# Inverse root mean squares of the second layer's q and k: one GpSimd power operation in place of eleven VectorE links

## The chip, the cores and the metric

The kernel runs on one core of a Trainium2 chip. A core has a matrix engine (TensorE, PE in the profile), three engines for elementwise work (VectorE, DVE; ScalarE, ACT; GpSimd, POOL) and a queue for transfers (SyncE, SP). Each works down its own list of instructions in order; semaphores tie the lists together. The metric is the device time in microseconds (us); less is better.

## What is computed

Two transformer layers on 16 sequences ("batches" here) of 512 tokens with 128 features, 16 heads of 8 features. The part that the change touches is the normalisation of q and k in the second layer: each head's 8 values are divided by the root of their mean square.

```python
def rms_norm(x, w):
    xf = x.astype(jnp.float32)
    rms = jnp.sqrt(jnp.mean(xf * xf, axis=-1, keepdims=True) + EPS)
    return (xf / rms * w.astype(jnp.float32)).astype(x.dtype)
...
q = rms_norm(q, qn_w)
k = rms_norm(k, kn_w)
scores = jnp.einsum('bhsd,bhtd->bhst', q, k) * scale
attn = jax.nn.softmax(scores, axis=-1)
out = jnp.einsum('bhst,bhtd->bhsd', attn, v)
...
x = x + _L0_attn_ref(_layernorm(x), ...)
x = x + _L0_ffn_ref(_layernorm(x), ...)
x = x + _L1_attn_ref(_layernorm(x), ...)
x = x + _L1_ffn_ref(_layernorm(x), ...)
```

## The kernel before, in words

**Tiling and stages.** 32 attention passes follow each other: layer 0 and layer 1 of the 16 batches, interleaved as (0, b), (1, b-2). A pass is 64 units. One unit is a score tile of 128x512 for the exponential (TensorE, then `exp` on ScalarE into `probs`) and, 26 units ahead, a score tile for the row maxima (TensorE, then a maximum reduction on VectorE into `neg_max`). After each four units TensorE multiplies `probs` with the values. There are three score banks for each of the two uses, so TensorE can be at most three tiles ahead of VectorE or ScalarE. Everything else (projections, norms, the gated network, routing) is cut into pieces and put between the units.

**What sets the order.** Each engine has a table of due times, in units: `PE_AT`, `ACT_AT`, `DVE_AT`, `POOL_AT`, `SP_AT`. A program loop over `TIMES` writes the instructions of an engine in the order of these times; at run time only semaphores and the list itself hold an instruction. A due time is therefore a place in a list and no clock time: an engine that has nothing ahead starts as soon as its semaphores allow.

**q and k of the second layer.** TensorE computes them by token (`qka`, `qkb`), VectorE adds a bias into `qk1` (`take_qk1`), ScalarE squares them into `sq`, which lies in the buffer `ht`. `inverse_rms` on VectorE then does 14 steps, `nw0` to `nw13` in the table: two sums over 8 values (`ms`, 128x64 each), mean and epsilon, and eleven Newton links on 128x128 tiles (a shift, a subtraction for the first guess, three rounds of three). Each link waits for the one before by the semaphore `newton` and stands alone between two maxima. `scale_qk` on GpSimd multiplies `qk1` with the result `nw_y` in eight instructions, four for q and four for k. TensorE transposes the scaled q and k (pieces `qt` and `kt`, line L1125, `ps<-ident,qk` in the profile); ScalarE and GpSimd split them in bfloat16 parts (`part0`, `residual1`, `part1`, `residual2`), and SyncE sends the parts through memory into `q_stack` and `k_stack`, from which the next attention pass of layer 1 is fed.

**What stands around it on GpSimd.** `normalise` (L589) multiplies the attention output `o_raw`, in two halves, with the inverse denominators; these come by a transfer into `rden_all`, after a reciprocal on VectorE (L927). The half 0 of a pass stands ahead of the scaling, half 1 behind it. TensorE's projection `pr0` or `pr1` (L1201) waits for both. `norm_factors` (L570, L572) raises variances (`vpe`, 128x4) to the power -0.5 with the constant tile `half_neg` and multiplies; ScalarE's normalisation L696 waits for it. On VectorE `parts_high` (the cast L899) and `parts_low` (L908) stand after each sixteen maxima.

Of the kernel before, what the change touches and what calls it, by code (L numbers as in the profile page):

```python
# [7 lines left out]
I32 = mybir.dt.int32  # L8
ALU = mybir.AluOpType
ACT = mybir.ActivationFunctionType  # L10
AX = mybir.AxisListType

BATCH, SEQ, D = 16, 512, 128
HEADS, HD = 16, 8
TT = SEQ // 128
# [5 lines left out]
LN_EPS, RMS_EPS = 1e-5, 1e-6  # L21
# [57 lines left out]
SP_AT = {"A": {"rows0": -5, "rows1": 10, "rows2": 23, "rows3": 46, "den0": 40, "rden0": 55, "den1": 66,  # L79
                "rden1": 74},  # L80
# [40 lines left out]
PE_DUE, ACT_DUE, DVE_DUE, POOL_DUE, SP_DUE = (due_table([t]) for t in (PE_AT, ACT_AT, DVE_AT, POOL_AT, SP_AT))  # L121
# [5 lines left out]
def at(due, name, t):  # L127

    return due[name][t] if name in due and t in due[name] else None
# [51 lines left out]
def need(eng, sem, value):  # L181

    if value > 0:
        eng.wait_ge(sem, value)


def build(nc, T, out_dram):
    ctx = ExitStack()
    with ctx:
        def sb(name, shape, dt=F32):  # L190
            return ctx.enter_context(nc.sbuf_tensor(name, shape, dt))

        def sem(name):
            return ctx.enter_context(nc.semaphore(name))
# [23 lines left out]
        w_mid = sb("w_mid", [128, 2 * EXPERTS])  # L218
        mid_bias = sb("mid_bias", [128, 2 * EXPERTS])
        w_lora = sb("w_lora", [EXPERTS * RANK + 1, D])  # L220
        half_neg = sb("half_neg", [128, TT])

        x_in = sb("x_in", [128, TT, D])
        res = [[sb(f"res{l}{k}", [128, TT, D]) for k in range(l + 1)] for l in (0, 1)]
# [5 lines left out]
        vpe = [sb(f"vpe{k}", [128, TT]) for k in range(4)]  # L230
        rstd = [sb(f"rstd{k}", [128, TT]) for k in range(4)]
# [24 lines left out]
        qk1 = sb("qk1", [128, TT, 2 * D])  # L256
        sq = ht[:, 0:2, :].rearrange("p c (t n) -> p (c t) n", n=2 * D)
        ms = sb("ms", [128, TT * 32])
        nw_y = sb("nw_y", [128, TT * 32])
        nw_t = sb("nw_t", [128, TT * 32])  # L260
        nw_u = sb("nw_u", [128, TT * 32])

        rm = sb("rm", [128, TT, 2 * EXPERTS])
        lmax = sb("lmax", [128, TT])
# [48 lines left out]
        rstd_ready = [sem(f"rstd_ready{k}") for k in range(4)]  # L313
# [25 lines left out]
        tanh_done = sem("tanh_done")  # L339
        ht_done = sem("ht_done")  # L340
        squared = sem("squared")
        newton = sem("newton")
        qk_normed = [sem(f"{c}_normed") for c in "qk"]
        moe = sem("moe")
        l_exp = sem("l_exp")
# [1 line left out]
        gate_ready = sem("gate_ready")  # L347
        coef_ready = sem("coef_ready")
        stored = sem("stored")
        N_NEWTON = 14  # L350

        def v_of(l, b):
            return v_aug[l][b % 2 if l == 1 else 0]
# [192 lines left out]
        def _(pool):  # L546
# [20 lines left out]
            def norm_factors(k, b):  # L567

                pool.wait_ge(var_ready[k], b + 1)
                pool.tensor_tensor(rstd[k][:, :], vpe[k][:, :], half_neg[:, :], ALU.pow).then_inc(rstd_ready[k], 1)  # L570
                pool.wait_ge(rstd_ready[k], b + 1)
                pool.tensor_tensor(shift[k][:, :], neg_mean[k][:, :], rstd[k][:, :], ALU.mult).then_inc(shift_ready[k], 1)  # L572

# [12 lines left out]
            def normalise(l, c, b):  # L586
# [2 lines left out]
                pool.tensor_tensor(o_of(l, b)[:, c, :], o_of(l, b)[:, c, :], rden_all[:, c, :], ALU.mult  # L589
                                   ).then_inc(att_ready[l], 1)  # L590

            def scale_qk(n, b):

                if n == 0:
                    pool.wait_ge(newton, N_NEWTON * (b + 1))
                x = qk1[:, :, D * n:D * n + D].rearrange("p t (h e) -> p t h e", e=HD)
                inv = nw_y[:, :].rearrange("p (t n h) -> p t n h", t=TT, n=2)[:, :, n, :]
                for t in range(TT):
                    last = pool.tensor_tensor(x[:, t, :, :], x[:, t, :, :], wide(inv[:, t, :, None], 2, HD), ALU.mult)
                last.then_inc(qk_normed[n], 1)  # L600
# [25 lines left out]
            clear_values(v_aug[1][0], 2)  # L626
            clear_values(v_aug[1][1], 3)
            for t in TIMES:
                for n in (0, 1):
                    b = at(POOL_DUE, f"sc{n}", t)  # L630
                    if b is not None:
                        scale_qk(n, b)
                a = at(POOL_DUE, "no1", t)
                if a is not None:
                    normalise(a[0], 1, a[1])
                b = at(POOL_DUE, "nf1", t)
                if b is not None:
                    norm_factors(1, b)
                for c in range(NH):
                    b = at(POOL_DUE, f"um{c}", t)  # L640
                    if b is not None:
                        up_mul(c, b)
                for l in (1, 0):
                    for n in (0, 1):
                        b = at(POOL_DUE, f"r1_{'qk'[n]}{l}", t)
                        if b is not None:
                            residual1(l, n, b)
                        b = at(POOL_DUE, f"r2_{'qk'[n]}{l}", t)
                        if b is not None:
                            residual2(l, n, b)  # L650
                b = at(POOL_DUE, "nf3", t)
                if b is not None:
                    norm_factors(3, b)
                b = at(POOL_DUE, "mix", t)
                if b is not None:
                    mix(b)
                b = at(POOL_DUE, "nf0", t)
                if b is not None:
                    norm_factors(0, b)
                b = at(POOL_DUE, "nf2", t)  # L660
                if b is not None:
                    norm_factors(2, b)
                a = at(POOL_DUE, "no0", t)
                if a is not None:
                    normalise(a[0], 0, a[1])
# [177 lines left out]
        def _(dve):  # L843
# [110 lines left out]
                    last = dve.tensor_tensor(qk1[:, 2 * half + t, :], gen[:, 256 * t:256 * t + 256], qk1_bias[:, :], ALU.add)  # L954
                last.then_inc(read[name], 1)

            def inverse_rms(first, count, b):

                for n in range(first, first + count):
                    if n < 2:  # L960
                        dve.wait_ge(squared, 2 * b + n + 1)
                        op = dve.tensor_reduce(ms[:, 64 * n:64 * n + 64],
                                               sq[:, 2 * n:2 * n + 2, :].rearrange("p t (g e) -> p (t g) e", e=HD),
                                               AX.X, ALU.add)
                    else:
                        dve.wait_ge(newton, N_NEWTON * b + n)
                        if n == 2:
                            op = dve.tensor_scalar(ms[:, :], ms[:, :], 1.0 / HD, RMS_EPS, ALU.mult, ALU.add)
                        elif n == 3:
                            op = dve.tensor_scalar(nw_t[:, :].bitcast(I32), ms[:, :].bitcast(I32), 1, None,  # L970
                                                   ALU.logical_shift_right)
                        elif n == 4:
                            op = dve.tensor_scalar(nw_y[:, :].bitcast(I32), nw_t[:, :].bitcast(I32), -1.0,
                                                   float(0x5f3759df), ALU.mult, ALU.add)
                        elif n % 3 == 2:
                            op = dve.tensor_tensor(nw_t[:, :], nw_y[:, :], nw_y[:, :], ALU.mult)
                        elif n % 3 == 0:
                            op = dve.scalar_tensor_tensor(out=nw_u[:, :], in0=nw_t[:, :], scalar=-0.5, in1=ms[:, :],
                                                          op0=ALU.mult, op1=ALU.mult)
                        else:  # L980
                            op = dve.scalar_tensor_tensor(out=nw_y[:, :], in0=nw_u[:, :], scalar=1.5, in1=nw_y[:, :],
                                                          op0=ALU.add, op1=ALU.mult)
                    op.then_inc(newton, 1)

            def route(link, b):

# [41 lines left out]
            for t in TIMES:  # L1028
# [5 lines left out]
                a = max_at(t - 1)  # L1034
                if a is not None and a[2] % 16 == 15:
                    parts_low(a[0], a[2] // 16, a[1])
                for n in range(N_NEWTON):
                    b = at(DVE_DUE, f"nw{n}", t)
                    if b is not None:
                        inverse_rms(n, 1, b)  # L1040
                for l in (1, 0):
                    for part in (0, 1):
                        b = at(DVE_DUE, f"tv{l}{'ab'[part]}", t)
# [6 lines left out]
                b = at(DVE_DUE, "add1", t)  # L1050
                if b is not None:
                    project_add(1, x3, b)
                b = at(DVE_DUE, "st3a", t)
# [3 lines left out]
                b = at(DVE_DUE, "st3b", t)  # L1057
                if b is not None:
                    stats(3, x3, b, (2, 3))
                b = at(DVE_DUE, "mo3", t)  # L1060
                if b is not None:
                    moments(3, b)
                b = at(DVE_DUE, "fa3", t)
                if b is not None:
                    factors_in(3, b)
                for link in range(3):
                    b = at(DVE_DUE, f"ro{link}", t)
                    if b is not None:
                        route(link, b)
                for link in range(3):  # L1070
                    b = at(DVE_DUE, f"ga{link}", t)
                    if b is not None:
                        gates(link, b)
                b = at(DVE_DUE, "fin", t)
                if b is not None:
                    finish(b)
                b = at(DVE_DUE, "st0a", t)
# [3 lines left out]
                b = at(DVE_DUE, "st0b", t)  # L1081
# [237 lines left out]
```

## Time and profile before

| | us |
|---|---|
| median of three runs | 2039.22 |
| lowest and highest run | 2016.17, 2040.07 |
| the profiled execution's own time | 2025.97 |
| its span | 2024.2 |
| mean granted TensorE clock in it | 0.954 of 2.4 GHz |

The rows further down come from this one profiled execution. Times in them are us from the start of the span; durations of grouped instructions are means in ns. An instruction's duration begins before the one ahead of it on the same engine has quite ended, so that a row's end is up to 0.1 us behind the next row's start. "PEclk" is the granted clock of TensorE as a share of 2.4 GHz: 1.00 is 2.4 GHz and 0.50 is 1.2 GHz. Lines such as L893 are those of the kernel.

### The profile page before, as it was taken

The numbers are of one execution on the slowest core, as the hardware profiler recorded it, in microseconds if no ns is written. First come the engines' busy times: TensorE is split into PE (matmuls) and PEld (weight loads), VectorE is DVE, ScalarE is ACT, GpSimd is POOL, SyncE is SP. The second block draws the span as 40 slices with busy tenths as digits, with TensorE's granted clock in tenths as the row PEclk, the third lists the DMA queues.
The fourth block names the chain that finished last, engine by engine and source line by source line (L and its number), as shares of the span: only waits on it lengthen the run. The fifth ranks groups of instructions, "written<-read, shape, count | busy, mean of one in ns | idle before, by whom it ended". The sixth has DMA issues, their size and how long they took to land.

```text
span 2024.2 us, 32134 instructions
## 1 busy us (share of the span) xinstructions
PE 1763.1 (87%) x10958; PEld 650.9 (32%) x10958; DVE 1604.7 (79%) x3587; ACT 1431.4 (71%) x2921; POOL 438.1 (22%) x579
## 2 busy tenths in 40 slices
PE   4998898989989898998988889898988989898895
PEld 1232332323233232333333233332423323233233
DVE  3978786887988888787887969887797877786871
ACT  2777676776877777676786857777687776666773
POOL 3122112131222213112122311213121221222201
PEclk8899997999999999999999989999999989899987
DMA  6223405032050513205041240504205042022310
GB/s 120 59 71 82 99 24 137 18 114 51 24 146 14 140 27 87 79 24 142 18 120 46 63 103 13 148 18 111 54 23 143 18 112 48 19 80 59 80 34 22
DMA packets 162644, 141.34 MB, mean 70 GB/s; under 512 B 38761, under 2 KB 144050, under 8 KB 162482
## 3 DMA queue, kind: packets, MB, share of 16 engines
q1 hardware_dynamic: 162482, 139.29, 26.6%
q8 instruction: 88, 1.44, 0.3%
q14 instruction: 74, 0.61, 0.1%
HBM read 77.38 MB, written 55.57 MB: 66 GB/s over the span
## 4 chain that ended last, share of the span: by engine, by line
PE 36%; DVE 23%; DMA 14%; ACT 13%; issue 5%; SPq 5%; POOL 5%; DVEq 0%; POOLq 0%; ACTq 0%
DVE neg_max L893 15%; PE ps L1175 11%; PE ps L1160 7%; PE ps L1196 6%; ACT probs L690 6%; DMA rden_all<-rden_rows 4%; DMA q_stack<-m_parts 3%; DMA k_stack<-k_rows 3%; ACT xn L696 3%; PE ps L1149 3%; PE ps L1125 2%; PE ps L1240 2%; PE ps L1201 2%; DMA k_rows<-kp 2%; SPq L424 2%
## 5 line engine op out<-in xcount | busy, mean ns | idle before, releaser
L893 DVE TENSOR_REDUCE neg_max<-ps 128x1 f32<-128x512 f32 x2048 | 1314.9, 680 | 208.0 <-PE ps L1149 203.3
L690 ACT ACTIVATE probs<-ps 128x512 f32<-128x512 f32 x2048 | 1098.4, 595 | 362.6 <-PE ps L1160 361.6
L1149 PE MATMUL ps<-k_stack,q_stack 48*128 48x512 bf16 x2048 | 699.1, 397 | 81.2 <-DMA k_stack<-k_rows 38.7
L1160 PE MATMUL ps<-q_stack,k_stack 50*128 50x512 bf16 x2048 | 672.2, 393 | 76.5 <-ACT probs L690 31.2
L1175 PE MATMUL ps<-probs,v_aug 128*32 128x512 f32 x4096 | 567.6, 627 | 0.1
L1160 PEld LDWEIGHTS ps<-q_stack,k_stack 50*128 50x128 bf16 x2048 | 153.2, 94 | 614.6 <-ACT probs L690 386.4
L1149 PEld LDWEIGHTS ps<-k_stack,q_stack 48*128 48x128 bf16 x2048 | 157.5, 94 | 223.7 <-DVE neg_max L893 158.1
L589 POOL TENSOR_TENSOR o_raw<-o_raw,rden_all 128x512 f32<-128x512 f32 x64 | 81.7, 1276 | 664.9 <-DMA rden_all<-rden_rows 664.9
L1175 PEld LDWEIGHTS ps<-probs,v_aug 128*32 128x32 f32 x4096 | 81.6, 109 | 156.4 <-issue 110.0
L570 POOL TENSOR_TENSOR rstd<-vpe,half_neg 128x4 f32<-128x4 f32 x64 | 64.5, 1008 | 297.3 <-DVE vpe L884 297.3
L696 ACT ACTIVATE xn<-x,shift,rstd 128x128 f32<-128x128 f32 x192 | 81.0, 491 | 32.3 <-POOL shift L572 32.3
L613 POOL TENSOR_TENSOR coef<-gating,rm 128x64 f32<-128x64 bf16 x64 | 16.8, 295 | 329.8 <-DVE gating L1009 329.8
L606 POOL TENSOR_TENSOR ht<-up,gs 128x512 f32<-128x512 f32 x48 | 61.0, 1271 | 122.3 <-ACT up L671 122.3
L1201 PE MATMUL ps<-wo,o_raw 128*128 128x128 f32 x512 | 72.6, 300 | 12.9 <-POOL o_raw L589 12.3
L1201 PEld LDWEIGHTS ps<-wo,o_raw 128*128 128x128 f32 x512 | 66.3, 209 | 33.4 <-issue 32.3
L1125 PE MATMUL ps<-ident,xn 128*128 128x128 f32 x256 | 47.2, 313 | 32.4 <-ACT xn L696 30.7
L931 DVE TENSOR_TENSOR x<-ps,res 128x512 f32<-128x512 f32 x32 | 22.1, 691 | 61.6 <-PE ps L1201 61.6
L943 DVE SCALAR_TENSOR_TENSOR gs<-th,ps 128x512 f32<-128x512 f32 x48 | 33.0, 688 | 40.2 <-ACT th L740 38.2
L1196 PE MATMUL ps<-xnt,w_gate 128*128 128x256 f32 x192 | 54.3, 405 | 9.8 <-ACT xnt L671 3.7
L671 ACT ACTIVATE up<-ps 128x512 f32<-128x512 f32 x48 | 28.7, 597 | 47.4 <-PE ps L1196 47.4
L931 DVE TENSOR_TENSOR x<-ps,x 128x512 f32<-128x512 f32 x32 | 22.0, 688 | 45.4 <-PE ps L1240 28.3
L1196 PE MATMUL ps<-xnt,w_up 128*128 128x256 f32 x192 | 54.3, 405 | 2.8 <-DVE gs L943 2.6
(103 smaller groups left out, 1503.7 us busy)
## 6 DMA issues: line engine op xcount, KB each, us to landing
q_stack<-q_rows SPq DMA_DIRECT2D x128, 192.0 KB, 3.8
k_stack<-k_rows SPq DMA_DIRECT2D x128, 192.0 KB, 4.8
rden_all<-rden_rows SPq DMA_DIRECT2D x64, 256.0 KB
q_rows<-qp SPq DMA_DIRECT2D x32, 384.0 KB, 2.6
k_rows<-kp SPq DMA_DIRECT2D x32, 384.0 KB, 3.5
q_rows<-qp SPq DMA_DIRECT2D x32, 256.0 KB, 3.1
k_rows<-kp SPq DMA_DIRECT2D x32, 256.0 KB, 3.2
x_in<-in_L_attn_x SPq DMA_DIRECT2D x16, 256.0 KB, 3.1
```

The lines of the kernel that those rows point to most:

```text
L570: pool.tensor_tensor(rstd[k][:, :], vpe[k][:, :], half_neg[:, :], ALU.pow).then_inc(rstd_ready[k], 1)
L589: pool.tensor_tensor(o_of(l, b)[:, c, :], o_of(l, b)[:, c, :], rden_all[:, c, :], ALU.mult).then_inc(att_ready[l], 1)
L606: pool.tensor_tensor(ht[:, c, :], up[:, :], gs[:, :], ALU.mult).then_inc(ht_done, 1)
L690: act.activation(probs[:, g % RING, :], ps[:, g % BANKS, :], ACT.Exp).then_inc(exps, 1)
L696: last = act.activation(xn[k][:, t, :], x[:, t, :], ACT.Identity, bias=shift[k][:, t:t + 1], scale=rstd[k][:, t:t + 1])
L893: dve.tensor_reduce(neg_max[l][:, pair // 2, col:col + 1], ps[:, BANKS + g % BANKS, :], AX.X, ALU.max, negate=True).then_inc(max_taken, 1)
L1125: return pe.transpose(dst, src, ident[0:n, 0:n])
L1149: pe.matmul(ps[:, BANKS + g % BANKS, :], q_stack[l][row:row + KROWS, pair, tok:tok + 128], k_stack[l][row:row + KROWS, pair, :], start=Tru ...
L1160: pe.matmul(ps[:, g % BANKS, :], k_stack[l][row:row + AROWS, pair, tok:tok + 128], q_stack[l][row:row + AROWS, pair, :], start=True, stop= ...
L1175: last = pe.matmul(acc[32 * j:32 * j + 32, :], v_of(l, b)[:, kt, 8 * e + 2 * group + pp, :], probs[:, (g + j) % RING, :], start=(s == 0 an ...
L1196: return pe.matmul(gen[:, 256 * half:256 * half + 256], w, xt[:, 256 * half:256 * half + 256], start=True, stop=True)
L1201: last = pe.matmul(gen4[:, t, :], o_of(l, b)[:, c, 128 * t:128 * t + 128], wo[l][:, c, :], start=c == 0, stop=c == 1)
```

## The change

VectorE keeps the two sums and the step for mean and epsilon, now `ms0` to `ms2` in the table at the due times of the first three steps (55, 57, 59); the eleven links go. GpSimd gets one `tensor_tensor` with the operation power, `ms` (128x128) to the power of `half_neg`, into a new tile `inv_rms`. `half_neg` grows from 128x4 to 128x128 for it. The new operation's place in GpSimd's table is 3 of the group M2, ahead of the scaling at 7, and the scaling waits for its semaphore `inv_ready`. VectorE's first sum of the next batch waits for the same semaphore.

```diff
@@ -63,9 +63,7 @@
-                "mo2": 45, "tqa": 54, "tqb": 55, "nw0": 55, "nw1": 57, "nw2": 59, "nw3": 60, "nw4": 61,
...
+                "mo2": 45, "tqa": 54, "tqb": 55, "ms0": 55, "ms1": 57, "ms2": 59},
@@ -74,7 +72,7 @@
-           "M2": {"sc0": 7, "sc1": 7, "r1_q1": 11, "r2_q1": 22, "r1_k1": 19, "r2_k1": 22},
+           "M2": {"pw": 3, "sc0": 7, "sc1": 7, "r1_q1": 11, "r2_q1": 22, "r1_k1": 19, "r2_k1": 22},
@@ -218,7 +216,7 @@
-        half_neg = sb("half_neg", [128, TT])
+        half_neg = sb("half_neg", [128, TT * 32])
@@ -567,7 +564,7 @@
-                pool.tensor_tensor(rstd[k][:, :], vpe[k][:, :], half_neg[:, :], ALU.pow).then_inc(rstd_ready[k], 1)
+                pool.tensor_tensor(rstd[k][:, :], vpe[k][:, :], half_neg[:, 0:TT], ALU.pow).then_inc(rstd_ready[k], 1)
@@ -589,12 +586,16 @@
+            def inverse_rms(b):
+
+                pool.wait_ge(mean_sq, N_MS * (b + 1))
+                pool.tensor_tensor(inv_rms[:, :], ms[:, :], half_neg[:, :], ALU.pow).then_inc(inv_ready, 1)
+
             def scale_qk(n, b):
 
-                if n == 0:
-                    pool.wait_ge(newton, N_NEWTON * (b + 1))
+                pool.wait_ge(inv_ready, b + 1)
                 x = qk1[:, :, D * n:D * n + D].rearrange("p t (h e) -> p t h e", e=HD)
-                inv = nw_y[:, :].rearrange("p (t n h) -> p t n h", t=TT, n=2)[:, :, n, :]
+                inv = inv_rms[:, :].rearrange("p (t n h) -> p t n h", t=TT, n=2)[:, :, n, :]
@@ -954,33 +958,18 @@
-            def inverse_rms(first, count, b):
...
-                        elif n % 3 == 2:
-                            op = dve.tensor_tensor(nw_t[:, :], nw_y[:, :], nw_y[:, :], ALU.mult)
-                        elif n % 3 == 0:
-                            op = dve.scalar_tensor_tensor(out=nw_u[:, :], in0=nw_t[:, :], scalar=-0.5, in1=ms[:, :],
-                                                          op0=ALU.mult, op1=ALU.mult)
-                        else:
-                            op = dve.scalar_tensor_tensor(out=nw_y[:, :], in0=nw_u[:, :], scalar=1.5, in1=nw_y[:, :],
-                                                          op0=ALU.add, op1=ALU.mult)
-                    op.then_inc(newton, 1)
+            def mean_square(n, b):
+
+                if n < 2:
+                    dve.wait_ge(squared, 2 * b + n + 1)
+                    need(dve, inv_ready, b)
+                    op = dve.tensor_reduce(ms[:, 64 * n:64 * n + 64],
+                                           sq[:, 2 * n:2 * n + 2, :].rearrange("p t (g e) -> p (t g) e", e=HD),
+                                           AX.X, ALU.add)
+                else:
+                    dve.wait_ge(mean_sq, N_MS * b + n)
+                    op = dve.tensor_scalar(ms[:, :], ms[:, :], 1.0 / HD, RMS_EPS, ALU.mult, ALU.add)
+                op.then_inc(mean_sq, 1)
```

The first place where the order of instructions moves is GpSimd's list around the scaling. This is the list of before, in the middle of the program:

```order
L570 TENSOR_TENSOR rstd0<-vpe0,half_neg 128x4
L572 TENSOR_TENSOR shift0<-neg_mean0,rstd0 128x4
L589 TENSOR_TENSOR o_raw10<-o_raw10,rden_all 128x512
L599 TENSOR_TENSOR qk1<-qk1,nw_y 128x128 x8
L589 TENSOR_TENSOR o_raw10<-o_raw10,rden_all 128x512
L577 TENSOR_TENSOR qf1<-qf1,qp1 128x512
L577 TENSOR_TENSOR kf1<-kf1,kp1 128x512
```

And this is the same place in the changed kernel, whose line numbers are others:

```order
L567 TENSOR_TENSOR rstd0<-vpe0,half_neg 128x4
L569 TENSOR_TENSOR shift0<-neg_mean0,rstd0 128x4
L586 TENSOR_TENSOR o_raw10<-o_raw10,rden_all 128x512
L592 TENSOR_TENSOR inv_rms<-ms,half_neg 128x128
L600 TENSOR_TENSOR qk1<-qk1,inv_rms 128x128 x8
L586 TENSOR_TENSOR o_raw10<-o_raw10,rden_all 128x512
L574 TENSOR_TENSOR qf1<-qf1,qp1 128x512
```

The power stands between half 0 of `o_raw` and the scaling; half 1 and the splitting of q and k stay behind the scaling. The second place is VectorE's list between the sums of squares and the cast after sixteen maxima, in the kernel before:

```order
L968 TENSOR_SCALAR ms<-ms 128x128
L893 TENSOR_REDUCE neg_max0<-ps 128x1
L970 TENSOR_SCALAR nw_t<-ms 128x128
L893 TENSOR_REDUCE neg_max0<-ps 128x1
L973 TENSOR_SCALAR nw_y<-nw_t 128x128
L893 TENSOR_REDUCE neg_max0<-ps 128x1
L976 TENSOR_TENSOR nw_t<-nw_y 128x128
L893 TENSOR_REDUCE neg_max0<-ps 128x1
L978 SCALAR_TENSOR_TENSOR nw_u<-nw_t,ms 128x128
L893 TENSOR_REDUCE neg_max0<-ps 128x1
L981 SCALAR_TENSOR_TENSOR nw_y<-nw_u,nw_y 128x128
L893 TENSOR_REDUCE neg_max0<-ps 128x1 x2
```

In the changed kernel the same place reads:

```order
L971 TENSOR_SCALAR ms<-ms 128x128
L897 TENSOR_REDUCE neg_max0<-ps 128x1 x7
L931 RECIPROCAL rden1<-den1 128x32
L897 TENSOR_REDUCE neg_max0<-ps 128x1 x3
L903 CAST neg_high0<-neg_max0 128x16
```

The links between the maxima are gone. In the list of before the reciprocal L927 follows the last row shown, so five links stand ahead of it and six behind.

## Rows read from the trace of the kernel before

**Rows 1.** The page: busy time by engine, and the chain that ended last.

```profile
PE 1763.1 (87%) x10958; PEld 650.9 (32%) x10958; DVE 1604.7 (79%) x3587; ACT 1431.4 (71%) x2921; POOL 438.1 (22%) x579
...
PE 36%; DVE 23%; DMA 14%; ACT 13%; issue 5%; SPq 5%; POOL 5%; DVEq 0%; POOLq 0%; ACTq 0%
```

**Rows 2.** Busy time by stretch: stretch, length, then each engine, clock, DMA.

```profile
998.90:1011.70 12.80, 11.15 (x69) 2.83 (x67) 12.77 (x32) 9.60 (x21) 1.27 (x1) 1.00 0.07 24
```

**Rows 3.** The chain in order of time (start, us on the chain, what), batch 7.

```profile
999.70 0.13 DVE nw_t L970
...
1001.16 0.20 DVE nw_t L976
...
1010.24 0.79 DVE nw_u L978
```

**Rows 4.** Timeline of GpSimd, batch 7: start, us, operation, idle time before it.

```profile
1009.61 1.27 POOL L589 TENSOR_TENSOR o_raw<-o_raw,rden_all 128x512 f32<-128x512 f32 x1 [19.72 <-DMA rden_all<-rden_rows]
1011.91 2.96 POOL L599 TENSOR_TENSOR qk<-qk,nw_y 128x128 f32<-128x128 f32 x8 [1.02 <-DVE nw_y L981]
1029.08 1.27 POOL L589 TENSOR_TENSOR o_raw<-o_raw,rden_all 128x512 f32<-128x512 f32 x1 [14.20 <-DMA rden_all<-rden_rows]
```

**Rows 5.** Timeline of TensorE, batch 7: q taken, and the projection behind it.

```profile
1025.83 0.66 PE L1125 MATMUL ps<-ident,qk 128*128 128x128 f32 x4
...
1030.85 2.05 PE L1201 MATMUL ps<-wo,o_raw 128*128 128x128 f32 x16
```

**Rows 6.** GpSimd's groups by shape: count, busy us, mean ns, idle before and releaser.

```profile
L570 POOL TENSOR_TENSOR rstd<-vpe,half_neg 128x4 f32<-128x4 f32 x64 | 64.5, 1008 | 297.3 <-DVE vpe L884 297.3
L599 POOL TENSOR_TENSOR qk<-qk,nw_y 128x128 f32<-128x128 f32 x128 | 47.4, 411 | 42.6 <-DVE nw_y L981 42.6
L572 POOL TENSOR_TENSOR shift<-neg_mean,rstd 128x4 f32<-128x4 f32 x64 | 13.0, 203 | 5.0
```

**Rows 7.** Timelines of GpSimd and TensorE: scaling and q taken, batches 1 and 12.

```profile
283.94 1.14 POOL L599 TENSOR_TENSOR qk<-qk,nw_y 128x128 f32<-128x128 f32 x3 [1.02 <-DVE nw_y L981]
297.87 0.66 PE L1125 MATMUL ps<-ident,qk 128*128 128x128 f32 x4
...
1614.05 2.96 POOL L599 TENSOR_TENSOR qk<-qk,nw_y 128x128 f32<-128x128 f32 x8 [1.02 <-DVE nw_y L981]
1627.97 0.66 PE L1125 MATMUL ps<-ident,qk 128*128 128x128 f32 x4
```

**Rows 8.** Timeline of GpSimd, batch 13.

```profile
1737.28 2.96 POOL L599 TENSOR_TENSOR qk<-qk,nw_y 128x128 f32<-128x128 f32 x8 [1.02 <-DVE nw_y L981]
1746.28 1.01 POOL L570 TENSOR_TENSOR rstd<-vpe,half_neg 128x4 f32<-128x4 f32 x1 [6.03 <-DVE vpe L884]
```

**Rows 9.** Timeline of TensorE: two of its longest waits.

```profile
1165.89 0.61 PE L1149 MATMUL ps<-k_stack,q_stack 48*128 48x512 bf16 x2 [3.86 <-DMA k_stack<-k_rows]
...
1651.44 0.61 PE L1149 MATMUL ps<-k_stack,q_stack 48*128 48x512 bf16 x2 [4.43 <-DMA k_stack<-k_rows]
```

**Rows 10.** Maxima L893 by stretch: length, VectorE's time and count, granted clock, DMA.

```profile
1166.00:1182.00 16.00, 8.19 (x13) 0.50 0.48 144
1047.10:1063.10 16.00, 13.67 (x22) 1.00 0.63 177
1651.40:1660.00 8.60, 4.04 (x6) 0.50 0.90 241
```

**Rows 11.** Timelines of GpSimd and VectorE at 1038 us.

```profile
1038.31 1.16 POOL L583 TENSOR_TENSOR qp<-qf,qp 128x512 bf16<-128x512 f32 x1
1038.44 1.05 DVE L883 TENSOR_SCALAR neg_mean<-mv 128x4 f32<-128x4 f32 x1
```

**Rows 12.** Timelines of VectorE's cast and of GpSimd, two places.

```profile
1019.27 0.17 DVE L899 CAST neg_high<-neg_max 128x16 bf16<-128x16 f32 x1
...
1074.85 1.01 POOL L570 TENSOR_TENSOR rstd<-vpe,half_neg 128x4 f32<-128x4 f32 x1 [9.73 <-DVE vpe L884]
...
1075.40 0.17 DVE L899 CAST neg_high<-neg_max 128x16 bf16<-128x16 f32 x1
```

More of the change, by code:

```diff
@@ L258, in build @@
         ms = sb("ms", [128, TT * 32])
-        nw_y = sb("nw_y", [128, TT * 32])
-        nw_t = sb("nw_t", [128, TT * 32])
-        nw_u = sb("nw_u", [128, TT * 32])
+        inv_rms = sb("inv_rms", [128, TT * 32])
         rm = sb("rm", [128, TT, 2 * EXPERTS])
@@ L341, in build @@
         squared = sem("squared")
-        newton = sem("newton")
+        mean_sq = sem("mean_sq")
+        inv_ready = sem("inv_ready")
         qk_normed = [sem(f"{c}_normed") for c in "qk"]
@@ L349, in build @@
         stored = sem("stored")
-        N_NEWTON = 14
+        N_MS = 3
         def v_of(l, b):
@@ L628, in _ @@
             for t in TIMES:
+                b = at(POOL_DUE, "pw", t)
+                if b is not None:
+                    inverse_rms(b)
                 for n in (0, 1):
@@ L955, in take_qk1 @@
                 last.then_inc(read[name], 1)
-            def inverse_rms(first, count, b):
[L959 to L964, printed above, removed]
-                    else:
[L966 to L974, printed above, removed]
-                        elif n % 3 == 2:
-                            op = dve.tensor_tensor(nw_t[:, :], nw_y[:, :], nw_y[:, :], ALU.mult)
-                        elif n % 3 == 0:
-                            op = dve.scalar_tensor_tensor(out=nw_u[:, :], in0=nw_t[:, :], scalar=-0.5, in1=ms[:, :],
-                                                          op0=ALU.mult, op1=ALU.mult)
-                        else:
-                            op = dve.scalar_tensor_tensor(out=nw_y[:, :], in0=nw_u[:, :], scalar=1.5, in1=nw_y[:, :],
-                                                          op0=ALU.add, op1=ALU.mult)
-                    op.then_inc(newton, 1)
@@ L1036, in _ @@
                     parts_low(a[0], a[2] // 16, a[1])
-                for n in range(N_NEWTON):
-                    b = at(DVE_DUE, f"nw{n}", t)
+                for n in range(N_MS):
+                    b = at(DVE_DUE, f"ms{n}", t)
                     if b is not None:
-                        inverse_rms(n, 1, b)
+                        mean_square(n, b)
                 for l in (1, 0):
```

2 rows, old and new, of the table DVE_AT are left out of this document.

## Prediction

> **What bounds the kernel now.** I read the page first. Its busy line gives TensorE 87%, VectorE 79%, ScalarE 71% and GpSimd 22% of 2024.2 us, and the chain that ended last takes 36% of the span on TensorE, 23% on VectorE and only 5% on GpSimd [rows 1]. No engine bounds the whole: one unit of attention (one score tile for the maximum, one for the exponential) goes round TensorE, VectorE and ScalarE in turn, and every engine works down a fixed list. So a place decides, not an average.
>
> The change sits in two places. The first is the stretch of Newton links. From 998.9 to 1011.7 us (batch 7) VectorE is busy for 12.77 of 12.80 us, TensorE for 11.15, ScalarE for 9.60 [rows 2], and the chain in order of time runs here through VectorE: a maximum, a link of 0.13 or 0.20 us, a maximum, a link [rows 3]. Here a link costs the whole machine its time. The second place is the GpSimd list. It finishes `o_raw` of half 0 at 1009.61+1.27 = 1010.9, waits 1.02 us for the last link, scales q and k in 2.96 us, and then has nothing to do for 14.2 us [rows 4]. TensorE asks for the scaled q only at 1025.83 [rows 5].
>
> **What the change removes.** Eleven links per batch. On the chain an integer link holds VectorE for 0.13 us, a multiplying one for 0.20, and the one that runs into `o_raw` on GpSimd for 0.79 [rows 3]. Two of 0.13, eight of 0.20 and one of 0.79 make 2.65 us a batch, 42 us in all as an upper bound. TensorE is busy 11.15 of the 12.80 us, so it would soon bound the stretch itself: I take 35 us if nothing else changes, 25 to 42.
>
> **What it adds.** One power of 128x128 elements on GpSimd, a shape that the trace does not have. It has the same operation on 128x4: 1008 ns in the mean of 64 [rows 6]. A multiply of the same 128x4 takes 203 ns and one of 128x128 takes 411 [rows 6]; one of 128x512 takes 1.27 us [rows 4]. So GpSimd has a fixed part of about 0.2 us and a slope of some 2.1 ns an element, and the power costs 805 ns more than the multiply for four elements. The question is whether these 805 ns are paid once or per element.
> - Lower bound, paid once: 0.411+0.805 = 1.2 us.
> - Per element, 805/4 = 201 ns each: 0.411+128x0.201 = 26.2 us.
> - Upper bound, the whole 1008 ns in proportion: 32x1.008 = 32.3 us.
>
> I take 26.2. GpSimd's other operations differ in slope and hardly in their fixed part, so an operation that is this much dearer at four elements is dearer by its arithmetic, and arithmetic is done for each element. Nothing in the trace excludes a long start-up.
>
> **Where it lies.** The new operation stands behind `o_raw` of half 0 and ahead of the eight scalings and of `o_raw` of half 1 (the first excerpt of the order), so it starts at 1010.9, not when the mean squares are ready at 999.1. It ends at 1037.1, and the first four scalings (half of 2.96) at 1038.6. TensorE wants q at 1025.83: it stands for 12.8 us, and with it, since every list is in order, VectorE and ScalarE. `o_raw` of half 1 then ends at 1041.3; TensorE's next user of it came 5 us behind q in the old trace (1030.85 against 1025.83 [rows 5]) and comes at 1043.6 now, so this costs nothing more. Batches 1 to 12 all show this distance: in the first the scaling starts at 283.94 and q is taken at 297.87, in the last 1614.05 and 1627.97 [rows 7]. The break-even is a power of 14.95-1.5 = 13.4 us, about 100 ns an element: anything shorter is hidden and the kernel gains, anything longer is paid in full 16 times.
>
> In batch 13 the scaling starts at 1737.28 and so the power at about 1736.3, and the norm factors of another batch stand right behind (1746.28 [rows 8]). They would come at 1736.3+26.2+3.0 = 1765.5, 19 us late. ScalarE and TensorE take their result a few us later; with that slack I put 5 us more on this batch. For the first batch and the last two I take the same 12.8.
>
> So 16x12.8+5 = 210 us are lost. Of the removed links only those ahead of the chain to `o_raw` of half 0 still help, five a batch, those before the reciprocal of the denominators in VectorE's list (the second excerpt of the order): 2x0.13+3x0.20 = 0.86 us [rows 3], 14 us in all. The rest only lets TensorE arrive sooner at a wait. That leaves +196.
>
> **The clock after each stall.** A TensorE that stands loses clock. Where it waited 3.86 us (to 1165.89) and 4.43 us (to 1651.44) for `k_stack` [rows 9], the granted clock behind was 0.50, 1.2 GHz, for 16 and 8.6 us more [rows 10]. At 0.50 VectorE did 13 maxima in 16 us, and 22 at full clock in the same place of an earlier pair of batches [rows 10]: 41% of the pace is gone. A stall of 12.8 us is longer than either. I add the shorter one, 8.6x0.41 = 3.5 us, for each of 16, 56 us; the bounds are 0 and 16x0.41 = 6.6 a batch, 105 us.
>
> Sum: 196+56 = +252 against the profiled execution's own time, 2025.97 us: 2278. The three runs shown lie at 2016, 2039 and 2040, and the same sum on their median gives 2291; I say **2285**.
>
> **The rivals.**
> 1. *The power is cheap, and the kernel gets no slower.* The 805 ns are start-up; the operation ends before 1024.3. Then the links are simply gone: 2026-35 = 1991 us, between 1984 and 2001, 1.2 to 2% faster. It decides at 13.4 us of length. For it: four elements are a thin base to go by, and no row excludes a long start-up. Against it: the multiply's start-up, 0.2 us. [...]
> 2. *The long operation also blocks VectorE.* Some VectorE operations wait for GpSimd to finish: `neg_mean` took 1.05 us for four elements a partition when it met a 1.16 us operation of GpSimd, and both ended at 1039.5 [rows 11]. Yet next to a power that began at 1074.85 and took its 1.01 us a cast at 1075.40 took 0.17 [rows 12], as the cast at 1019.27 does that meets nothing. In batch 7 a cast stands at 1019.27 [rows 12], 8.4 us behind the start of the power. If it is held until the end, VectorE stands for 17.8 us and TensorE stops at most three maxima (2 us) later: 3 to 5 us more a batch, 48 to 80 in all, 2335 to 2365 us. The Trainium skill (Advanced Engine Details and Errata, GPSIMD Details) says that the two engines share a read and a write interface and conflict when VectorE uses two ports or two SBUF inputs; by it this happens, and the `neg_mean` row agrees.
> 3. *In between.* Part start-up, part slope, 13.4 to 22 us: 2030 to 2210.
>
> That the operation would not replace the links is excluded: the order shows all eleven gone and one power in each batch.
>
> **How the numbers follow.** Power of 22 us or more without a block 0.45, with a block 0.21, in between 0.14, cheap 0.20. The forecast is the first. A range of 2045 to 2400 leaves out the cheap case and a sliver at the top and holds about 0.8; the upper end is 2285 and the 32.3 us operation (6x16 = 98) and some of the block. The slow case alone would be 2200 to 2400. About 2% is what a measurement of this kernel can tell from no change. Slower by over 2%: 0.45+0.21 and 0.12 of the middle, 0.78. Within 2%: the rest of the middle and most of the cheap case, 0.15. Faster by over 2%: 0.07, the cheap case when all 42 us come out.
>
> **What would show it.** The new operation's row: its mean, above all above or below 13.4 us. The waits: TensorE at the transposes of `qk` on GpSimd, some 12 us for each batch; none if the power is cheap. The granted clock: the mean under 0.954, with low stretches that begin in these stalls. VectorE: casts of over 5 us mean the block. If TensorE's wait is there but much shorter than 12 us with a power of 26 us, I have misread where it starts.

## The result, and the profile after

The changed kernel is slower: 2122.85 us median of four runs (2120.86 to 2134.0) against 2027.7 us for the kernel before (four runs, 2014.74 to 2040.07). The ratio is 1.0455, 95% interval 1.0405 to 1.0506, some 92 us. The direction was forecast and the time lies within the range, which was wide, but the forecast was 2285 us, +252 on the profiled execution. The profiled execution after took 2123.08 us, 97 more than the one before: the forecast loss is 2.6 times the one that came. The lines below are from this execution.

The page of the changed kernel: busy time by engine, and the chain that ended last, by engine and by line.

```profile
PE 1763.1 (83%) x10958; PEld 653.2 (31%) x10958; DVE 1562.9 (74%) x3411; ACT 1431.5 (67%) x2921; POOL 769.6 (36%) x595
...
PE 33%; POOL 21%; ACT 15%; DVE 14%; DMA 10%; issue 5%; SPq 2%; DVEq 0%; POOLq 0%; ACTq 0%
POOL inv_rms L592 16%; PE ps L1164 9%; DVE neg_max L897 9%; ACT probs L694 7%; PE ps L1149 6%; PE ps L1185 5%; ACT xn L700 4%; PE ps L1114 3%; DMA rden_all<-rden_rows 3%; DMA q_stack<-m_parts 3%; PE ps L1138 2%; PE ps L1229 2%; PE ps L1190 2%; DMA k_stack<-k_rows 2%; DVE bn L873 2%
```

Against [rows 1], TensorE does the same work in a longer span, VectorE has 42 us less, GpSimd 331.5 more, and GpSimd goes from 5% to 21% of the chain, 16% of it the new power alone. The groups of the power by shape, from the same kernel (busy us, mean ns, idle before):

```profile
L592 POOL TENSOR_TENSOR inv_rms<-ms,half_neg 128x128 f32<-128x128 f32 x16 | 332.5, 20781 | 5.2 <-DVE ms L971 5.2
...
L567 POOL TENSOR_TENSOR rstd<-vpe,half_neg 128x4 f32<-128x4 f32 x64 | 64.5, 1007 | 293.6 <-DVE vpe L888 293.6
```

A power of 128x128 takes 20.78 us where I took 26.2 [rows 6]. (Measured from its start to the start of the scaling behind it, it is 20.85 to 20.87 us in all 16 batches.) Batch 7 on GpSimd's timeline (start, us, operation, idle before), the place of [rows 4]:

```profile
1056.45 1.27 POOL L586 TENSOR_TENSOR o_raw<-o_raw,rden_all 128x512 f32<-128x512 f32 x1 [18.85 <-DMA rden_all<-rden_rows]
1057.67 20.79 POOL L592 TENSOR_TENSOR inv_rms<-ms,half_neg 128x128 f32<-128x128 f32 x1
1078.54 2.95 POOL L600 TENSOR_TENSOR qk<-qk,inv_rms 128x128 f32<-128x128 f32 x8
1081.45 1.27 POOL L586 TENSOR_TENSOR o_raw<-o_raw,rden_all 128x512 f32<-128x512 f32 x1
```

And TensorE's timeline there, the place of [rows 5]: the last work before q, and q itself.

```profile
1070.20 1.06 PE L1164 MATMUL ps<-probs,v_aug 128*32 128x512 f32 x8
1080.18 1.09 PE L1114 MATMUL ps<-ident,qk 128*128 128x128 f32 x4 [8.91 <-POOL qk L600]
```

TensorE stands for 8.91 us. The view of waits has it for the whole kernel, with the waits for `k_stack` (total us, times, longest):

```profile
PE ps L1114 <- POOL qk L600: 134.0, 15, 9.5
...
PE ps L1138 <- DMA k_stack<-k_rows: 23.6, 15, 5.9
...
PE ps L1114 <- ACT m_parts L675: 18.2, 1, 18.2
```

The waits for `k_stack` in the kernel before:

```profile
PE ps L1149 <- DMA k_stack<-k_rows: 38.7, 14, 5.8
```

Fifteen stalls, 134 us; the sixteenth batch, 13, stalls elsewhere, for 18.2 us. That is 152 us of new standing for 97 us of time. So two things have to be explained: why the stalls are shorter than 12.8 us, and where 55 us went.

### The profile page after: what moved, and what is told of

Its sections match the earlier page's. It is cut to its first block, busy times and chain, and to the rows that moved or that the text cites. A ratio compares the mean times of both kernels' runs of the same rounds, so it can differ in the third digit from the quotient of the medians.

```text
span 2121.3 us, 32004 instructions
## 1 busy us (share of the span) xinstructions
PE 1763.1 (83%) x10958; PEld 653.2 (31%) x10958; DVE 1562.9 (74%) x3411; ACT 1431.5 (67%) x2921; POOL 769.6 (36%) x595
## 4 chain that ended last, share of the span: by engine, by line
PE 33%; POOL 21%; ACT 15%; DVE 14%; DMA 10%; issue 5%; SPq 2%; DVEq 0%; POOLq 0%; ACTq 0%
POOL inv_rms L592 16%; PE ps L1164 9%; DVE neg_max L897 9%; ACT probs L694 7%; PE ps L1149 6%; PE ps L1185 5%; ACT xn L700 4%; PE ps L1114 3%; DMA rden_all<-rden_rows 3%; DMA q_stack<-m_parts 3%; PE ps L1138 2%; PE ps L1229 2%; PE ps L1190 2%; DMA k_stack<-k_rows 2%; DVE bn L873 2%
## 5 line engine op out<-in xcount | busy, mean ns | idle before, releaser
L592 POOL TENSOR_TENSOR inv_rms<-ms,half_neg 128x128 f32<-128x128 f32 x16 | 332.5, 20781 | 5.2 <-DVE ms L971 5.2
L1114 PE MATMUL ps<-ident,qk 128*128 128x128 f32 x128 | 33.9, 417 | 134.4 <-POOL qk L600 134.0
L723 ACT ACTIVATE qf<-ps,qn_scaled 128x512 f32<-128x512 f32 x16 | 11.0, 687 | 139.0 <-PE ps L1114 139.0
L1114 PEld LDWEIGHTS ps<-ident,qk 128*128 128x128 f32 x128 | 22.0, 210 | 161.3 <-issue 148.9
```

The costliest lines, as they stand in the source:

```text
L592: pool.tensor_tensor(inv_rms[:, :], ms[:, :], half_neg[:, :], ALU.pow).then_inc(inv_ready, 1)
L1114: return pe.transpose(dst, src, ident[0:n, 0:n])
```

## The experiments

**How long a power is.** At the very end of GpSimd's list of the kernel before:

```diff
+            for w, op in ((1, ALU.pow), (2, ALU.pow), (4, ALU.pow), (8, ALU.pow), (16, ALU.pow), (32, ALU.pow),
+                          (64, ALU.pow), (128, ALU.pow), (256, ALU.pow), (4, ALU.mult), ...):
+                pool.tensor_tensor(wide_out[:, at0:at0 + w], base[:, 0:w], expo[:, 0:w], op)
```

> The kernel before with a row of extra GpSimd operations at the very end: powers of 1 to 256 elements a partition, multiplies of 4 to 256, one power on 16 partitions and one on the last batch's mean squares. The time of the whole says nothing. Theory 'per element': the changed kernel's trace gives (20.78-1.008)/124 = 0.159 us an element and a fixed part of 0.37 us, so one element takes about 0.53 us, 16 take 2.9, 64 take 10.6, 256 take 41.2, on a straight line. Theory 'in steps' (elements done in groups of four or more, which would explain why four elements read dearer, 201 ns each, than 128): 1, 2 and 4 elements all take about 1.0 us and the line has steps. Both: 16 partitions take as long as 128, and real mean squares as long as a constant.

The groups of these operations by shape (busy us, mean ns). Where a group has x2 from 4 elements on, one is the power and one a multiply of the same shape.

```profile
L677 POOL TENSOR_TENSOR wide_out<-base,expo 128x256 f32<-128x256 f32 x2 | 42.0, 20976 | 0.0
L677 POOL TENSOR_TENSOR wide_out<-base,expo 128x128 f32<-128x128 f32 x2 | 21.2, 10618 | 0.0
L679 POOL TENSOR_TENSOR wide_out<-base,expo 16x128 f32<-16x128 f32 x1 | 20.8, 20762 | 0.0
L682 POOL TENSOR_TENSOR wide_out<-ms,expo 128x128 f32<-128x128 f32 x1 | 20.8, 20762 | 0.0
...
L677 POOL TENSOR_TENSOR wide_out<-base,expo 128x32 f32<-128x32 f32 x1 | 5.4, 5427 | 0.0
L677 POOL TENSOR_TENSOR wide_out<-base,expo 128x16 f32<-128x16 f32 x1 | 2.9, 2900 | 0.0
L677 POOL TENSOR_TENSOR wide_out<-base,expo 128x8 f32<-128x8 f32 x1 | 1.6, 1637 | 0.0
...
L677 POOL TENSOR_TENSOR wide_out<-base,expo 128x2 f32<-128x2 f32 x1 | 0.7, 705 | 0.0
L677 POOL TENSOR_TENSOR wide_out<-base,expo 128x1 f32<-128x1 f32 x1 | 0.5, 549 | 0.0
```

A straight line without steps: 705-549 = 156 ns for the second element, (5427-2900)/16 = 158 for each from 16 to 32, and (20762-5427)/96 = 160 for each from 32 to 128. At 158 ns an element the fixed part is 549-158 = 0.39 us. Partitions don't matter (16 take as long as 128), nor do the values. So the power's fixed part is 0.39 us and not the multiply's 0.2. I had put this 0.19 us into the slope of a row of four elements, which made the slope some 42 ns an element too high, and 128 elements made 5.4 us of it.

**The links alone, and the stall alone.** The first kernel has neither links nor power (a multiply of constants stands for it, the inverse roots are left out); the second keeps the links and adds the power, whose result nobody uses.

```diff
 links_gone, against the changed kernel
-                pool.tensor_tensor(inv_rms[:, :], ms[:, :], half_neg[:, :], ALU.pow).then_inc(inv_ready, 1)
+                pool.tensor_tensor(inv_rms[:, :], half_neg[:, :], half_neg[:, :], ALU.mult).then_inc(inv_ready, 1)
 links_kept, against the kernel before
                 if n == 0:
+                    pool.wait_ge(newton, N_NEWTON * b + 3)
+                    pool.tensor_tensor(inv_rms[:, :], ms[:, :], exps_neg[:, :], ALU.pow).then_inc(inv_ready, 1)
                     pool.wait_ge(newton, N_NEWTON * (b + 1))
```

> The changed kernel with the power replaced by a multiply of constants of the same shape, 0.4 us; the inverse roots are left out, q and k are multiplied by 0.25. It measures the removal of the eleven links alone. By the chain, 2.65 us a batch, of which I took 35 us in all: 1985 to 2000 us, ratio to the kernel before 0.98 to 0.985. By the traces of the changed kernel and of the early power the second-layer pass in which the links lie is only 1.7 to 2.1 us shorter: 27 to 34 us, ratio 0.983 to 0.987, and less where the clock takes it back.

> The kernel before with the power added behind o_raw half 0, its result unused, and the scaling behind it; all links stay. It measures the stall alone. The power of 20.8 us and the first half of the scaling end 22.3 us behind o_raw half 0, TensorE wants q at 14.95: 7.4 us in 12 batches, about the same in three more and some 12 in batch 13, 120 to 130 us if nothing takes any back, 2150 to 2160 us. If TensorE's lost clock were paid in full on top (5 us at half clock behind each stall, about 2 us lost each) it would be 2180 or more. If the waits for k_stack absorb it and shrink, as the traces suggest, 2130 to 2160.

Without links and power: 2004.33 us median, ratio 0.985 (0.9798 to 0.9902), 30 us saved (20 to 41 by the interval) where I had put 35. With links and power: 2135.46 us, ratio 1.0513 (1.0451 to 1.0575), 104 us lost, the last of the three cases expected. TensorE's timeline in the second, batch 7:

```profile
1076.80 1.09 PE L1132 MATMUL ps<-ident,qk 128*128 128x128 f32 x4 [7.38 <-POOL qk L605]
```

7.4 us had been expected, and 7.4 it is in all of batches 1 to 12. In the changed kernel the stall is 9 us because the removed links let TensorE arrive earlier at the same wait. So the links are worth 30 us alone and much less next to the power. How much less, the times don't settle: 104-92 = 12 us, with intervals of 13 and 10 us on the two terms (forecast: 14). By the profiled executions it is 2127.0-2121.3 = 6 us of span, and by the table below 0.66 us in each of batches 1 to 12.

**A power as long as I had assumed.**

```diff
+                pool.tensor_tensor(more_pow[:, :], ms[:, 0:32], half_neg[:, 0:32], ALU.pow)
                 pool.tensor_tensor(inv_rms[:, :], ms[:, :], half_neg[:, :], ALU.pow).then_inc(inv_ready, 1)
```

> The changed kernel with a second power of 32 elements ahead of each power, 5.5 us, so that the two together take 26.2 us, the length that the prediction assumed. Theory 'only the length was wrong': the rest of my sum, with 56 us for the lost clock, holds, and the time is 2270 to 2300 us. Theory 'the clock term was wrong too': each further microsecond of stall costs one microsecond and no more, 2123+16x5.5 = 2211 us, 2200 to 2225.

2214.31 us, ratio 1.0843 (1.0759 to 1.0926). The extra power takes 5.43 us by its group's mean, 87 us for 16, and costs (1.0843-1.0455)x2030 = 79 us. With exactly the 26.2 us of my sum the kernel is some 70 us below my 2285: the length was not the only error. Its profiled execution took 2215.98 us, 190 more than the one before. My sum has 196 without the term for the clock and 252 with it, so that term was the other error.

**Where the clock's loss goes.** The granted clock falls as I had said: its mean is 0.926 against 0.954, and the low stretches begin in the stalls. In the changed kernel, by stretch (length, TensorE busy, weights, VectorE, ScalarE, GpSimd, clock, DMA): the stall of batch 7, the 6.4 us behind it, and what follows.

```profile
1071.40:1080.10 8.70, 0.00 (x0) 0.00 (x0) 0.39 (x1) 0.81 (x2) 8.62 (x6) 0.79 0.19 60
1080.20:1086.60 6.40, 6.40 (x28) 2.25 (x30) 2.58 (x4) 4.76 (x9) 4.12 (x7) 0.50 0.01 3
1086.70:1100.00 13.30, 12.94 (x92) 5.03 (x88) 13.21 (x32) 10.38 (x21) 8.54 (x9) 1.00 0.69 189
```

But TensorE's next wait, for the `k_stack` of the pass that uses this q, shrinks. The changed kernel, and then the kernel before at the same place:

```profile
1100.64 0.39 PE L1138 MATMUL ps<-k_stack,q_stack 48*128 48x512 bf16 x1 [0.46 <-DMA k_stack<-k_rows]
```

```profile
1047.00 0.39 PE L1149 MATMUL ps<-k_stack,q_stack 48*128 48x512 bf16 x2 [2.20 <-DMA k_stack<-k_rows]
```

The distances between these places, worked out from the starts of TensorE's rows in each trace as means over batches 1 to 12, in us. "To q" is from the first score tile of the layer-0 pass to q; then from q to the first maximum tile of the layer-1 pass (in brackets the wait right before it), from there to that pass's first score tile, and that pass itself. The last two columns are the time at 0.50 of the clock within the second stretch and within the third.

| kernel | to q | q to maxima | to the pass | pass | sum | low clock, 2nd | low clock, 3rd |
|---|---|---|---|---|---|---|---|
| before | 11.92 | 21.81 (2.76) | 22.72 | 64.70 | 121.15 | 0.35 | 5.71 |
| changed | 21.04 | 20.69 (0.97) | 22.08 | 62.56 | 126.37 | 5.21 | 2.89 |
| links gone | 11.92 | 21.74 (2.62) | 23.79 | 62.21 | 119.66 | 0.52 | 8.90 |
| links kept, power added | 19.37 | 21.08 (1.17) | 21.25 | 65.32 | 127.03 | 5.55 | 0.58 |
| power of 26.2 us | 26.46 | 20.70 (0.93) | 22.04 | 63.07 | 132.26 | 6.14 | 2.60 |
| power early | 11.92 | 21.74 (2.75) | 25.09 | 62.99 | 121.74 | 0.27 | 12.69 |
| hybrid | 11.92 | 21.93 (2.67) | 24.00 | 62.61 | 120.45 | 0.66 | 9.60 |

The second stretch holds the lost clock, 5.2 us of it, and is not longer but 1.1 us shorter. The loss itself is real. Here is this stretch of batch 7 in the kernel before and in the changed one, in the same columns as the stretches above:

```profile
1025.83:1047.00 21.17, 16.98 (x123) 6.62 (x119) 18.13 (x39) 18.72 (x40) 11.45 (x11) 1.00 0.55 153
```

```profile
1080.18:1100.64 20.46, 19.64 (x119) 7.30 (x119) 16.43 (x37) 15.80 (x32) 12.79 (x15) 0.84 0.49 130
```

In the mean of batches 1 to 12 TensorE is busy for 16.93 us in it before and for 19.16 in the changed kernel, with the same 118 matmuls (counted by their starts). These 2.2 us for 4.9 us more of low clock are 0.46 of each, close to the 0.41 that I had read from [rows 10]. (TensorE's busy time rests on modelled ends of its matmuls.) But TensorE stands idle there for 1.53 us instead of 4.88. The wait for `k_stack` gives 1.8 us of that, and smaller waits, for `probs` and for another transfer into `q_stack`, give the rest. TensorE waits at the end of the stretch in each of the 12 batches, in both kernels, so its end is set by the transfer into `k_stack`, which starts 15.3 us behind q instead of 16.6. One part of this is that GpSimd begins to split q 2.9 us after TensorE took it instead of 4.5: `o_raw` half 1 stands ahead of the splitting, and in batch 7 it waited for its transfer before [rows 4] and doesn't in the changed kernel.

The third stretch goes from 5.71 to 2.89 us of low clock and is 0.6 us shorter. The wait ahead of it is not all that sets this: links gone, power early and hybrid wait there as long as the kernel before and have 9 to 13 us of low clock behind it. The fourth stretch has the removed links, 2.1 us. Over 12 batches that makes 109 us of later q, less 13, 8 and 26: 63 us. The rest of the 97 lies in the first batches (8) and the last (26). With links kept all this is seen without the links' part: 16 stalls of together 126 us cost 104. And links gone shows why its saving is below the upper bound: 2.5 us less in the pass, of which 1.1 come back in the third stretch with its longer low clock.

**The break-even.** The power on half of the elements (a multiply fills the rest, half of the inverse roots are left out):

```diff
-                pool.tensor_tensor(inv_rms[:, :], ms[:, :], half_neg[:, :], ALU.pow).then_inc(inv_ready, 1)
+                pool.tensor_tensor(inv_rms[:, 64:], ms[:, 64:], half_neg[:, 64:], ALU.mult)
+                pool.tensor_tensor(inv_rms[:, 0:64], ms[:, 0:64], half_neg[:, 0:64], ALU.pow).then_inc(inv_ready, 1)
```

> The changed kernel with the power on 64 of the 128 elements (the other half is a multiply, so half of the inverse roots are left out). The power stays behind o_raw half 0 and takes 10.5 us, under the 13.4 us that fit there. If the break-even was read rightly, TensorE waits for the scaled q nowhere but perhaps in the first and the last batches, and the time is that of the kernel with no power at all, within 1%. If a long GpSimd operation costs anything beyond its place in the list, it is over that by more than 1%.

```profile
L593 POOL TENSOR_TENSOR inv_rms<-ms,half_neg 128x64 f32<-128x64 f32 x16 | 168.8, 10549 | 0.0
```

2013.25 us, ratio 0.9898 (0.9844 to 0.9953), half a per cent above the kernel without any power, which is within the noise of both. Of 16 powers of 10.5 us none makes TensorE wait for q; the one stall left is batch 13's, 7.6 us, where the norm factors are late. Below 13.4 us the power is hidden, as read.

**The power earlier.** It need not stand behind `o_raw` half 0; the mean squares are ready some 11 us before.

```diff
-           "M2": {"pw": 3, "sc0": 7, "sc1": 7, ...
+           "M2": {"pw": -11, "sc0": 7, "sc1": 7, ...
```

> The changed kernel with the power's due time at -11 instead of 3, so that it stands in GpSimd's list ahead of o_raw half 0 and starts when the mean squares are ready, some 11 us earlier. Theory 'stall': the 16 stalls of about 9 us are the whole loss. The power then ends about 9 us behind where o_raw half 0 used to be ready, o_raw half 0 and the scaling come behind it, and q is scaled at about the moment TensorE wants it: stalls of 0 to 1.5 us, and the time falls from 2123 to 1985 to 2015 us, below the kernel before. Rival 'a long operation costs elsewhere' (shared memory ports, late o_raw): it stays above 2040.

GpSimd's timeline in this kernel, batch 7; TensorE takes q at 1031.88 and waits for nothing:

```profile
1007.57 20.78 POOL L592 TENSOR_TENSOR inv_rms<-ms,half_neg 128x128 f32<-128x128 f32 x1 [9.29 <-DVE ms L971]
1028.32 1.27 POOL L586 TENSOR_TENSOR o_raw<-o_raw,rden_all 128x512 f32<-128x512 f32 x1
1029.56 2.96 POOL L600 TENSOR_TENSOR qk<-qk,inv_rms 128x128 f32<-128x128 f32 x8
```

2048.07 us, ratio 1.0065 (1.0023 to 1.0107): 75 us better than the changed kernel, but not the 1985 to 2015 expected. It lies above 2040, which was the sign given for the rival. But neither cost that the rival names shows in the trace: 29 casts of VectorE under the power took 174 to 176 ns, and TensorE waits 11.6 us in all for `o_raw`, 12.3 before. What shows is this. Batches 1 to 12 have no stall; 0, 13, 14 and 15, whose lists are packed otherwise, still have 8.3, 6.8, 7.1 and 10.1 us, 32 in all. And its profiled execution has 12.7 us of low clock a batch behind the `k_stack` wait, where the kernel before has 5.7, and 2.4 us more in that stretch, which takes the links' gain back. Why the clock was low for longer there is open: the wait before it is the same, 2.75 us. Part of it differs from one execution to the next. This execution took 2060.61 us, 12.5 above the median, and the hybrid below, which does the same in batches 1 to 12, had 9.6 us.

**Both where each is better.** The early power for batches 1 to 12, the links for the other four:

```diff
+        LINKS = (0, 13, 14, 15)
...
+                if b is not None and b not in LINKS:
+                    inverse_pow(b)
```

> The early power (ahead of o_raw half 0) for batches 1 to 12, and the eleven links for batches 0, 13, 14 and 15, where the early power still left stalls of 8.3, 6.8, 7.1 and 10.1 us. If these four stalls are what keeps the early power above the kernel before, it saves about 30 us against it: 2010 to 2025 us, ratio 0.985 to 0.995 to the kernel before. If the rest of the lost gain goes elsewhere (longer stretches at 1.2 GHz behind the waits for k_stack), the ratio stays within 0.995 to 1.00.

2013.23 us (six runs, 2008.34 to 2017.34) against 2034.34, ratio 0.9898 (0.9859 to 0.9937), as expected if the four stalls were the loss: 1% faster than the kernel before, a small gain but clear of its interval, and the fastest of the kernels that compute everything. Against the early power it gains 34 us, give or take 12, for the 32 us of stalls that it takes out.

## Why the prediction was right or wrong

**What bounds the kernel, and the place of the change: right.** The power starts when `o_raw` half 0 ends, TensorE waits for q and nothing before it, and `o_raw` half 1 costs nothing more: TensorE waits for it 9.5 us in all, 12.3 before.

**The length of the power: the first error.** The step was "the power costs 805 ns more than the multiply for four elements", divided by four. It takes the fixed parts for equal; they are 0.39 and 0.2 us. That gives 158 to 160 ns an element instead of 201, 20.8 us instead of 26.2, 5.4 us a batch and 86 us in the sum. The bounds of 1.2 and 32.3 us held it, but 20.8 us is below the 22 us of the main case.

**The stall: right for its length.** By the same sum a power of 20.8 us gives 7.4 us, and 7.38 was measured with the links in place. In batch 13 I had put 17.8 us for the long power, which is 12.4 for the shorter one. With the links in place it is 13.9 us, so the slack that I gave it was 1.5 us too large; in the changed kernel, without them, it is 18.2.

**The removed links: right in kind.** Alone they gave 30 us (20 to 41) where 35 were forecast. Beside the stall 14 were forecast; the runs show that most of the gain goes into a longer stall (9.05 us against 7.38) and leave 6 to 12 us, within noise.

**The clock: the second error.** The step was "I add 8.6x0.41 = 3.5 us for each of 16". The clock fell and was at 1.2 GHz for 5.2 us behind q, not 8.6, and the price of it was as read: 2.2 us of longer work for TensorE. What failed is that this loss was added to the time in full. TensorE had 4.9 us of idle time between q and the next pass, 2.8 of them waiting for `k_stack`, a transfer that starts when q has gone through ScalarE and GpSimd. The longer work fell into this idle time, and the term was nothing, the lower bound that I had given it, or a small gain instead of 56 us. The power of 26.2 us shows it without the first error: +190 us in its profiled execution, against 196 forecast without the clock term and 252 with it. So +252 becomes 252-86-56 = +110; the two shorter stretches take 13 and 8 us off and batch 13 adds 18.2-12.4 = 6, which gives 95, against +97 in the profiled execution.

**The rivals.** What came is the third rival, "in between": a length between 13.4 and 22 us and a time between 2030 and 2210. I had given it 0.14. That the range held the time is due to its width, since it took in this case too, and not to the forecast case. The cheap power is out. The block of VectorE is out too: a cast at 1064.64 stood beside a power that had 14 us to go and took 0.17 us, as all 16 casts under a power did (174 to 177 ns).

```profile
1064.64 0.17 DVE L903 CAST neg_high<-neg_max 128x16 bf16<-128x16 f32 x1
1064.72 0.69 DVE L897 TENSOR_REDUCE neg_max<-ps 128x1 f32<-128x512 f32 x1
1065.32 0.17 DVE L912 TENSOR_TENSOR neg_max<-neg_max,neg_high 128x16 f32<-128x16 f32 x1
```

The Trainium skill (Advanced Engine Details and Errata, GPSIMD Details) says that GpSimd shares a read and a write interface with VectorE and conflicts with operations of VectorE in a two-port mode or with two SBUF inputs. Beside GpSimd's multiplies and subtractions the trace agrees: 14 operations at L912, which have two inputs, met one of these and took 0.59 to 1.11 us, as here in batch 7 of the changed kernel (VectorE, then GpSimd):

```profile
1088.97 0.59 DVE L912 TENSOR_TENSOR neg_max<-neg_max,neg_high 128x16 f32<-128x16 f32 x1
```

```profile
1088.38 1.15 POOL L580 TENSOR_TENSOR kp<-kf,kp 128x512 bf16<-128x512 f32 x1
```

Beside the power it doesn't: 16 operations of the same form took 165 to 168 ns. The measurement decides. Why the power doesn't hold them is open.

The Trainium skill (GPSIMD Engine Reference, Elementwise — side-by-side cycle accounting) gives about 2.6 cycles an element for an addition with two inputs, at 1.2 GHz an estimate of 2.2 ns. The multiplies here agree (2.1 ns). The power doesn't: the measurement decides, 158 ns.

## What to carry to other kernels

Take the slope of an unseen size from two sizes of the same operation; another operation's fixed part in its place is an error that the larger size multiplies. After a stall, look for idle time ahead that is set by something other than the slower engine before adding a cost: it may take the loss in. And a slow operation on an idle engine is worth its place in the list more than its length: 20.8 us cost 92 us behind one instruction, and ahead of it, in the batches where it fits, saved 1%.

## What the runs showed of the hardware

A GpSimd power takes 0.39 us and 158 to 160 ns an element a partition, the same for 16 and for 128 partitions and for constant and real values, some 75 times the slope of a multiply. While it runs it doesn't hold VectorE: casts take 174 to 177 ns and two-input operations 165 to 168 ns, where the latter take 0.59 to 1.11 us beside a GpSimd multiply or subtraction. The clock at 1.2 GHz costs TensorE 2.2 us of work for 4.9 us of it behind a stall, none of which reaches the time there. In the third stretch of the table it costs some 0.34 us of time for each us (power early against the kernel before, 2.37 us longer for 6.98 us more of low clock).
